# Two orders around the recurrent layer's norms: where ScalarE squares two blocks, and when GpSimd splits the second stage's first expert weights

## What is computed

```python
h = _layernorm(x) * (1 + ca) + sa                 # layer 0
x = x + ga * _L0_attn_ref(h, ...)                 # 16 heads, causal
h = _layernorm(x) * (1 + cb) + sb
x = x + gb * _L0_ffn_ref(h, ...)                  # 8 gelu experts, top 2, and a shared one
h = _layernorm(x) * (1 + ca) + sa                 # layer 1: "norm 2" of the kernel
x = x + ga * _L1_attn_ref(h, ...)                 # begins with an rms norm: "norm 3"
h = _layernorm(x) * (1 + cb) + sb                 # "norm 5"
x = x + gb * _L1_ffn_ref(h, ...)                  # 8 silu experts, top 2
```

## Time and profile before

| | |
|---|---|
| time, median of 3 runs | 679.75 us (679.01 to 680.6) |
| time of the profiled execution | 679.79 us |
| its span in the profile | 678.0 us |
| busy: TensorE, VectorE, ScalarE, GpSimd | 89%, 80%, 72%, 26% |
| mean granted TensorE clock | 0.949 |
| chain that ended last | TensorE 62%, VectorE 26%, ScalarE 5%, issue 5% |

### The profile page before, as it was taken

One profiled execution on the slowest core, in us unless ns is written; L12 is line 12 of the kernel. 1 busy time (PEld: TensorE's weight loads), 2 busy tenths in 40 slices (PEclk: granted clock), 3 DMA queues, 4 the chain that ended last, 5 costly groups with the idle time before them and its releaser, 6 DMA issues.

```text
span 678.0 us, 11084 instructions
## 1 busy us (share of the span) xinstructions
PE 606.8 (89%) x3284; PEld 441.1 (65%) x3284; DVE 545.4 (80%) x1345; ACT 486.1 (72%) x857; POOL 173.3 (26%) x147
## 2 busy tenths in 40 slices
PE   8788889888997899999999999782699899999996
PEld 5355556555545568888888887351385788888884
DVE  3667888888866658878888887756899689999997
ACT  4548999999553669999999998677635466666663
POOL 3422223332301415443554443310143000000000
PEclk9789999999996899999999999976699799999999
DMA  7000000000100120122202220000000042222201
GB/s 239 1 0 2 2 2 0 0 0 0 32 1 0 48 113 37 57 95 94 91 2 93 93 85 1 23 1 0 0 1 0 1 150 87 87 86 86 86 1 62
DMA packets 6651, 29.85 MB, mean 44 GB/s; under 512 B 887, under 2 KB 1024, under 8 KB 4417
## 3 DMA queue, kind: packets, MB, share of 16 engines
q1 hardware_dynamic: 6610, 29.37, 12.2%
HBM read 28.18 MB, written 1.19 MB: 43 GB/s over the span
## 4 chain that ended last, share of the span: by engine, by line
PE 62%; DVE 26%; issue 5%; ACT 5%; DMA 1%; SPq 0%; POOL 0%; DVEq 0%; ACTq 0%; POOLq 0%
PE PS L1127 16%; PE PS L1129 16%; PE PS L1128 16%; DVE STAT L802 8%; PE PS L1273 2%; DVE RA L822 2%; PE PS L1228 2%; DVE HN L656 2%; PE PS L1153 2%; DMA AR<-in_wmod 1%; DVE SU L828 1%; PE PS L1242 1%; DVE HN L652 1%; ACT RA L605 1%; DVE AR L1086 1%
## 5 line engine op out<-in xcount | busy, mean ns | idle before, releaser
L937 DVE TENSOR_TENSOR RA<-AR,RA 128x512 fp32r<-128x512 f32 x140 | 134.3, 983 | 29.1 <-ACT RA L509 28.4
L508 ACT ACTIVATE AR<-PS,BI 128x512 f32<-128x512 f32 x144 | 99.4, 691 | 26.2 <-PE PS L1129 16.6
L1127 PE MATMUL PS<-HH,WH 128*128 128x512 f32 x272 | 109.5, 403 | 0.1
L1129 PE MATMUL PS<-HL,WH 128*128 128x512 f32 x272 | 107.4, 395 | 0.0
L1128 PE MATMUL PS<-HH,WL 128*128 128x512 f32 x272 | 107.3, 395 | 0.0
L509 ACT ACTIVATE RA<-PS,BI 128x512 fp32r<-128x512 f32 x144 | 98.4, 683 | 0.0
L802 DVE CUSTOM_DVE_ANT_0 STAT<-PS,MQ 128x128 f32<-128x128 f32 (+1 forms) x256 | 76.3, 354 | 20.2 <-PE PS L1229 20.1
L1127 PE MATMUL PS<-RA,WH 128*128 128x512 f32 x208 | 82.4, 396 | 2.5 <-DVE RA L1093 2.1
L1129 PE MATMUL PS<-RA,WH 128*128 128x512 f32 x208 | 81.2, 391 | 0.0
L1128 PE MATMUL PS<-RA,WL 128*128 128x512 f32 x208 | 81.2, 390 | 0.0
L312 POOL TENSOR_TENSOR AR<-AR 128x512 f32<-128x512 f32 x32 | 51.2, 1601 | 111.9 <-DVE AR L756 111.9
(11 more groups left out here) (196 smaller groups left out, 1185.1 us busy)
## 6 DMA issues: line engine op xcount, KB each, us to landing
AR<-comb SPq DMA_DIRECT2D x16, 1024.0 KB, 4.6
WS<-in_w SPq DMA_DIRECT2D x9, 512.0 KB, 5.6
WS<-in_w SPq DMA_DIRECT2D x8, 384.0 KB, 3.1
M<-in_mats SPq DMA_DIRECT2D x1, 1384.0 KB, 12.2
X<-in_xT SPq DMA_DIRECT2D x4, 256.0 KB, 4.8
out_xT<-X SPq DMA_DIRECT2D x4, 256.0 KB, 2.1
AR<-in_wmod SPq DMA_DIRECT2D x1, 768.0 KB, 9.2
KM<-in_kmats SPq DMA_DIRECT2D x1, 162.5 KB
```

The source lines that it names most:

```text
L508: act.activation(G[:, c, :], PS[:, c, :], ACT.Gelu_apprx_tanh, bias=bias).then_inc(s["act"], 1)
L937: dve.tensor_tensor(out=GL[:, m0 % 2, c, :], in0=G[:, c, :], in1=f(GH[:, m0 % 2, c, :]), op=ALU.subtract).then_inc(s["lo"], 1)
L1127: pe.matmul(out, wh, xh, start=first, stop=False)
L1129: return pe.matmul(out, wh, xl, start=False, stop=last)
```

## The change

It has three parts. On ScalarE, square(3,2) moves ahead of inverse(2,3), and so into the place before a root that waits; square(3,3) stays between inverse(3,2) and inverse(3,3). On GpSimd, the two weight splits of the second stage move behind the four `split_hidden(3, ...)`. On SyncE, the call `later(8, 0)` is replaced by its first half: the load of expert 8's weights stays, the spreading of expert 8's routing weight, and the wait on VectorE's scaling ahead of it, are gone.

```diff
                 if ne == 9:
-                    later(8, 0)
+                    sp.wait_ge(s["split"], 16)
+                    sp.dma_start(WS[:, 0:width], w[8, :, :]).then_inc(s["w_in"], 16)
...
             gp.wait_ge(moe[0]["y"], 4 * E0)
+            for t in range(NBLK):
+                split_hidden(3, XC, t)
             for e in range(2):
                 gp.wait_ge(moe[1]["w_in"], 16 * (e + 1))
                 split_weights(1, e, e, 768)
-            for t in range(NBLK):
-                split_hidden(3, XC, t)
             for t in range(NBLK):
                 split_hidden(4, XC, t)
...
             square(2, XC, 3)
             inverse(3, 1)
+            square(3, HN, 2)
             inverse(2, 3)
-            for t in (2, 3):
-                square(3, HN, t)
-                inverse(3, t)
+            inverse(3, 2)
+            square(3, HN, 3)
+            inverse(3, 3)
```

## The result

The changed kernel takes 674.05 us (median of 11 runs, 672.44 to 678.09) against 678.51 us of the kernel before (11 runs, 675.47 to 681.92): a ratio of 0.9943, with a 95% interval of 0.9924 to 0.9961.

A forecast was written before the change was run, and what follows sets the result against it. A chain through engines was taken as the bound, with TensorE waiting 1.95 us ahead of variance(3,2). Square 1.80 plus splits 0.33 plus transfer 0 gave 2.13 us off 679.79; predicted 677.6 us, range 675.9 to 679.0.

The forecast's parts named there:

- the splits' 0.33 us: VectorE's multiplication of norm 2's block 0, freed from GpSimd's split, takes 0.68 us for 1.01: 0.33 us saved.
- the transfer's zero: Removing SyncE's spreading transfer, whose result no instruction reads, gains 0 us, with bounds at 0.38 us.
- The cover of the moved square: On ScalarE, the wait for variance(2,3) hides the moved square, costing 0.01 us; without it, up to 0.54 us.
- part 1: Moving the square of block 2 on ScalarE gives TensorE its input, and the Ln of (3,3), 1.80 us earlier.
- I take the same 5.91 us from the new start.: TensorE's run from variance(3,2) to the Ln of (3,3) keeps its length, with the clock rising 3.8 us in.
- The term of 1.80: Square of block 2 reaches TensorE at 443.08, not 444.88; all 1.80 us arrive, bounds 0.85 to 3.6.
- 1.0 us of slack: Square(3,3) on ScalarE ends at 447.08, TensorE reaches variance(3,3) at 448.09, so TensorE's run stays the limit.
- Its clock case: If TensorE's clock does not fall, square(3,3) becomes the limit and the Ln of (3,3) comes 3.6 us earlier.
- the clock gives more: Rival: TensorE's clock does not fall, or rises early, around the norms; 3.9 us gained, 675.9 us; chance 0.13.
- The clock takes part: Rival: the clock's rise does not move with TensorE's work; only 1.2 us gained, 678.5 us; chance 0.12.
- The contention rival: Rival: GpSimd's moved split goes ahead of VectorE's rest(3) of block 3, delaying it up to 2.64 us; 678.5; chance 0.05.
- the prediction's 0.13: VectorE's multiplication of norm 2's block 0 was 0.13 us shorter than the Skill's exclusion rule gives.

The follow-up runs named there:

- held clock: Extra idle matmuls in TensorE's gaps between the last gelus and the recurrence: 22 in the kernel before, ratio 0.9957; 16 in the changed kernel, ratio 0.9937.
- the two kernels that keep the old square: Kernel before with the splits moved and the spreading transfer gone, ratio 1.0006; kernel before with only the spreading transfer gone, ratio 0.9989.

## Why the prediction was wrong in size

**What held.** The sign and the place; the splits' 0.33 us, measured as 0.32 at VectorE's multiplication of block 1 and as 0.33 between the square alone at a clock that stayed up (35.64) and the full change at a held clock (35.31); the transfer's zero; and that what is gained at the Ln of (3,3) arrives: 3.15 us earlier there and at the recurrence, 3.28 at the MLP. The cover of the moved square held in the profiled execution (the root of (2,3) at most 0.1 us behind TensorE), but only because the clock was low there.

**The step that failed** is in part 1: "I take the same 5.91 us from the new start." The term of 1.80 was put down as a gap that closes at one clock, with the clock as a scatter to both sides. It is neither. From the start of variance(3,2) to the Ln of (3,3) it took 5.91 us before, about 5.1 in the changed kernel (447.64 - 442.51, the start of the Ln of (2,3)), and 4.56 with the square alone (445.28 - 440.72).

At one clock, the higher, the order is worth less than 1.80: 1.37 with the splits, and 36.68 - 35.64 = 1.04 alone. Two things make the difference. The old order's square of block 2 stood 18.55 us behind the mark at the held clock and 19.00 before, since the variance ahead of it was over sooner, so the move gains 1.34 there (18.55 - 17.21) and not 1.80. And 0.3 is lost again at variance(3,3), which waits for square(3,3). The prediction had given that square 1.0 us of slack, and had seen the slack go if the clock does not fall; what it did not see is that the moved square then also loses its cover and puts square(3,3) off by 0.44 us. It had priced this at "up to 0.54 us, on work that then has slack". The work had none. Its clock case had the Ln of (3,3) 3.6 us earlier; the square alone, at a clock that stayed up, measured 25.58 - 22.43 = 3.15.

The rest comes from the clock, and its mean goes one way. In the old order the low clock costs 38.81 - 36.68 = 2.13 us of the norm stretch (1.5 to 2.8 in the four executions), in the new one 36.11 - 35.31 = 0.80 (0.5 to 1.7 in five). So the 2.70 us are 1.37 of order and port, and 1.33 of clock; the last number rests on nine executions whose ranges overlap. In all four of the kernel before and in the two kernels that keep the old square the clock was low for 3.4 to 6.8 us; in the six of the new order without fillers for 0 to 3.4. The rival "the clock gives more" named this mechanism and had 0.13. That its 3.9 us are also the measured 3.9 is luck: it had them all in this stretch, which gave 2.7. "The clock takes part" had 0.12 and did not occur in any of the six. The two were weighed as if alike, though the change takes away an idle time of TensorE of 1.95 us.

**A part had no place in the prediction:** 0.78 us at the second stage's entry, over 80 us behind the edits. There the old order lost 1.5 us in two of four executions (in three of six with the two kernels that keep the old square), the new one in none of six without fillers. The clock explains each case. Which case it is stands already at the recurrence: in the three bad profiles the clock fell 1.7 to 1.8 us ahead of VectorE's first operation of the recurrence and stayed down for 23.9 us; in all the others of the table it fell from 0.4 us ahead of it to 1.5 us behind it, and stayed down for 20.5. In the new order it was 0.5 to 1.4 us behind each time. That an earlier recurrence brings the better case about is a guess that these rows agree with; it is not shown, since half of the old order's profiles had the better case too, and with so few executions a part of it may be chance.

**The contention rival** happened as to its cause and not its price. GpSimd did go first, by 0.06 us, and rest(3) of block 3 took 1.30 us; my argument that it would be slower than 0.04 us was wrong. The Trainium skill, page "SBUF — State Buffer", section "Who interferes with whom", has the second of two such operations wait for the first to end: 450.45 + 0.83 = 451.28 and then 0.69 of its own, as in the row of block 3 before, would be 451.97, against 451.81 in the trace. So here the rule agrees to 0.16 us, and the row is again the shorter, as with the prediction's 0.13. TensorE needed the result for the product that starts at 451.99 and had no gap, so the margin was 0.18 us, where 0.6 had been reckoned with. The splits themselves have room: their first reader starts at 527.68 in the trace of before, a little ahead of the 530 us said above.

## What to carry to other kernels

A gap in TensorE's work on a serial stretch is priced at least twice: what it is at one clock, and what the work around it costs if the gap lets the clock fall or puts off its rise; take both from rows at either level, and ask whether the edit makes TensorE more or less idle, since that gives the second term its sign. And a cover is to be worked out at the higher clock too: what waits for TensorE at 1.2 GHz may wait for nothing at 2.4. To tell order from clock, run both orders with harmless matmuls in the gaps. Such fillers were worth 0.43% on the old order by themselves, about as much as the reordering, and nothing measurable on top of it.

## What the runs showed of the hardware

The clock level differs from run to run of one kernel at the same instructions: one kernel spent 38.15, 38.78, 38.79 and 39.51 us in the same stretch. With ten extra matmuls around the second stage's entry the clock there was still down, for 6.8 us in place of 10.2, where with 16 in the norm stretch it was 1.00 throughout. A subtraction of 0.69 us on VectorE took 1.30 beside a GpSimd copy that began 0.06 us ahead of it, and GpSimd's subtraction behind that copy took 2.17 in place of 1.80. In this trace GpSimd, with its next operation ready, started it at 450.45, where the one before ended at 450.48 by its row, and VectorE, released by that end, started at 450.51.
